# A graph kernel's first gather stage: node features in two strided block loads, edge types as rows that TensorE spreads

## What is computed

```python
# first layer (R=32 types, B=8 basis matrices)
W_rel = einsum('rb,bdf->rdf', w_comp, weight)
agg   = segment_sum(h[src] * norm, etype * n_nodes + dst, 32 * n_nodes)
node  = einsum('rnd,rdf->nf', agg.reshape(32, n_nodes, 128), W_rel) + h_bias + h @ loop_weight
x     = layernorm(x + relu(node))
# second layer: per edge e = (x_dst - x_src) @ theta.T + x_src @ phi.T, batch norm, relu,
# @ fc1.T, batch norm, relu, mean over the edges of a destination, relu(. + x), layernorm
```

## Time and profile before

| | |
|---|---|
| median of 3 runs | 3090.55 us (3073.56 to 3092.17) |
| profiled execution | 3090.62 us |
| its span | 3088.8 us |
| mean granted TensorE clock | 0.712 |
| first gather stage, first gather to last | 11.4 to 1217.3 us |

### The profile page before, as it was taken

How to read it: one execution, slowest core, us unless ns; L and a number is a source line. 1 busy time by engine, 2 the same in 40 slices (tenths; PEclk the granted TensorE clock), 3 DMA queues, 4 the chain that set the end, 5 groups by cost and what they waited for, 6 DMA issues and landing times. The chain is left out here.

```text
span 3088.8 us, 42986 instructions
## 1 busy us (share of the span) xinstructions
PE 1948.1 (63%) x10210; PEld 1494.5 (48%) x10211; DVE 1365.8 (44%) x3584; ACT 614.7 (20%) x1004; POOL 1605.7 (52%) x1759
## 2 busy tenths in 40 slices
PE   2666566656666666635554545445555579999997
PEld 2555465645655556622222222222222234499996
DVE  4333333333433333533333333333333358877776
ACT  2111111111111111411010101010101137534434
POOL 5665665666666664246666666666666620092002
PEclk9778777778778787855555555555555569999999
DMA  3221212121222211223333333333333349534443
GB/s 87 54 55 53 59 51 56 52 60 54 59 59 53 59 54 40 90 86 95 103 99 94 96 95 93 95 108 96 95 94 96 108 178 308 185 121 143 145 149 96
DMA packets 124080, 291.20 MB, mean 94 GB/s; under 512 B 34957, under 2 KB 77506, under 8 KB 106224
## 3 DMA queue, kind: packets, MB, share of 16 engines
q1 hardware_dynamic: 65856, 136.12, 13.5%
q0 software_dynamic: 50048, 102.50, 12.8%
q10 hardware_dynamic: 8112, 51.91, 4.3%
HBM read 227.22 MB, written 63.18 MB: 94 GB/s over the span
## 5 line engine op out<-in xcount | busy, mean ns | idle before, releaser
L697 POOL DMA_INDIRECT G<-btab,srcT x782 | 737.5, 943 | 534.9 <-POOLq L56 278.6
L682 POOL DMA_INDIRECT G<-in_x,srcT x782 | 746.3, 954 | 469.1 <-issue 233.3
L906 PE MATMUL PS<-ident,G 128*128 128x128 f32 x784 | 212.9, 427 | 568.9 <-PEq L56 335.9
L906 PEld LDWEIGHTS PS<-ident,G 128*128 128x128 f32 x784 | 140.1, 217 | 662.5 <-issue 662.5
L791 PE MATMUL PS<-BIG 128*128 128x192 f32 (+1 forms) x1584 | 352.0, 372 | 126.4 <-issue 124.6
L780 PE MATMUL PS<-BIG,G 128*128 128x192 f32 x1564 | 362.9, 393 | 91.2 <-issue 57.6
L791 PEld LDWEIGHTS PS<-BIG 128*128 128x128 f32 x1584 | 312.8, 222 | 152.9 <-issue 152.6
L1477 DVE TENSOR_SCALAR ohT<-PS,node_col 80x512 bf16<-80x512 f32 x196 | 146.2, 746 | 536.6 <-DVEq L56 317.2
L780 PEld LDWEIGHTS PS<-BIG,G 128*128 128x128 f32 x1564 | 328.6, 237 | 105.3 <-issue 104.8
L1046 ACT ACTIVATE BIG<-PS 128x768 f32<-128x768 f32 x196 | 156.3, 809 | 1032.7 <-ACTq L56 887.4
L1313 DVE SCALAR_TENSOR_TENSOR BIG<-PS,dst0T,BIG 128x192 f32<-128x192 f32 x784 | 324.2, 416 | 79.9 <-issue 67.1
(11 more groups left out here) (182 smaller groups left out, 1834.3 us busy)
## 6 DMA issues: line engine op xcount, KB each, us to landing
BIG<-spill SPq DMA_DIRECT2D x90, 1024.0 KB, 4.9
spill<-BIG ACTq DMA_DIRECT2D x49, 1024.0 KB
G<-in_x,srcT POOLq DMA_INDIRECT x782
G<-btab,srcT POOLq DMA_INDIRECT x782
typ_i<-in_edge_type SPq DMA_DIRECT2D x97, 128.0 KB
BIG<-atab SPq DMA_DIRECT2D x196, 60.0 KB
atab<-BIG SPq DMA_DIRECT2D x12, 384.0 KB
xn<-in_x SPq DMA_DIRECT2D x48, 64.0 KB
```

The source lines that it names most:

```text
L682: nc.gpsimd.indirect_dma_start(out=G[0:n, g % 2, t, :], out_offset=None, in_=x, in_offset=bass.IndirectOffsetOnAxis(ap=srcT[0:n, TPG * g + ...
L697: nc.gpsimd.indirect_dma_start(out=G[0:n, g % 2, t, :], out_offset=None, in_=btab[:, :], in_offset=bass.IndirectOffsetOnAxis(ap=srcT[0:n, ...
L906: pe.matmul(PS[:, 2 + k, q * TILE:(q + 1) * TILE], G[:, h, TPC * k + q, :], ident[:, :], start=(q == 0), stop=False, is_transpose=True, sk ...
```

## The change

- **x**: xn is one buffer of 128 nodes. A new tile xh [128, 25, 128] receives x in two loads, blocks 0 to 24 behind the weights' loads in the setup, blocks 25 to 48 when 25 blocks have been used. Partition p holds the nodes 49 p to 49 p + 48, each load takes a contiguous run of each partition's nodes, and block g is therefore the nodes 49 p + g. ScalarE copies block g+1 from xh to xn (`next_x`), behind the copy of the transpose, which moves behind the fourth product's copy. XT and ACC keep their order by node; block g of them is now every 49th column (`every`).
- **edge types**: etype is loaded once as 98 rows beside src, dst and norm, and converted to bf16. TensorE spreads four rows over the 128 partitions by a product with a 0/1 matrix (`spread`, K = 98), 256 columns at a time, two products a group, into bank 7; VectorE makes the one-hots from PSUM, 256 columns at a time, two a group. typ_i and the 97 + 1 broadcast loads are gone.
- **order of TensorE in a group**: scaled sums 0; wait for the second one-hot of the group before (`rel_oh_ready`); [lookup of coefficients, odd groups], basis product 1; wait `loop_done`, first spreading; scaled sums 1; wait for x and for the first one-hot, transpose; basis product 0; loop product; second spreading.
- **order of VectorE**: half 0, first one-hot, half 1, add_loop, second one-hot. The coefficients are scaled in half 0 of the odd group. The lookup uses bank 5 instead of 4.

```diff
@@ SP
-            load_types(0, [ROW] * TPC)
+            def load_x(first, n):
+                for p0, p1 in ((0, EDGEP), (EDGEP, FULLP), (FULLP, P)):
+                    m = min(n, LASTW - first) if p1 == P else n
+                    of = x[p0 * NW + first:p0 * NW + first + m, :].rearrange("(p w) d -> p w d", p=1) if p1 == P else \
+                        x[p0 * NW:p1 * NW, :].rearrange("(p w) d -> p w d", w=NW)[:, first:first + n, :]
+                    sp.dma_start(xh[p0:p1, 0:m, :], of).then_inc(x_in, 16)
...
+            load_x(0, XH)
...
-            with sp.Fori(1, NG // 2 - 1) as i:
-                first_pass(2 * i, 0, i)
-                first_pass(2 * i + 1, 1, i)
...
+            take(sp, xw_free, XH)
+            load_x(XH, NW - XH)
+            sp.wait_ge(x_in, 16 * 6)
+            sp.sem_inc(x_here, NW - XH)
@@ TensorE
+            def spread_types(c, first, bank, at, n):
+                row = spread[:, bass.ds(c * TPC, TPC), :].rearrange("p q r -> p (q r)")
+                return pe.matmul(PS[:, bank, at:at + n], row, types[:, first:first + n], start=True, stop=True, skip_group_check=True)
...
+                    def first_types():
+                        take(pe, loop_done)
+                        spread_types(types_at[0], types_at[1], 7, 2 * P, QUARTER).then_inc(typ_spread, 1)
                     def turn_nodes():
-                        reached(pe, "pe", x_in[h], 16 * (use + 1))
-                        take(pe, loop_done)
-                        pe.transpose(PS[:, 7, 0:P], xn[:, h, 0:D], ident[:, :]).then_inc(xwT_ps, 1)
+                        take(pe, x_ready)
+                        take(pe, loop_done if last(g, NG) else rel_oh_ready)
+                        pe.transpose(PS[:, 7, 0:P], xn[:, :], ident[:, :]).then_inc(xwT_ps, 1)
...
+                    def second_types():
+                        spread_types(types_at[0], types_at[1] + QUARTER, 7, 2 * P, QUARTER).then_inc(loop_ps, 1)
...
                         if not (isinstance(g, int) and g == 0):
-                            basis_product(1, False)
+                            take(pe, rel_oh_ready)
+                            basis_product(1, h == 1)
+                        first_types()
+                        scaled_sums(g, h, use, 1)
                         turn_nodes()
-                        scaled_sums(g, h, use, 1)
-                        basis_product(0, h == 0)
+                        basis_product(0, False)
                         loop_product()
+                        second_types()
@@ ScalarE
-                    if k == (0 if last(g, NG) else 2):
+                    if k == (0 if last(g, NG) else CPG - 1):
                         take(act, xwT_ps)
                         act.sem_inc(xw_free, 1)
-                        act.activation(XT[:, bass.ds(g * TNODES, TNODES)], PS[:, 7, 0:P], ACT.Copy).then_inc(xwT_ready, 1)
+                        act.activation(every(XT, g), PS[:, 7, 0:P], ACT.Copy).then_inc(xwT_ready, 1)
+                        if not last(g, NG):
+                            next_x(g + 1)
@@ VectorE, setup
+            step(dve.tensor_copy(spread[:, :, :], ident[0:NR, 0:(NC + 1) * TPC].rearrange("p (n o) -> p n o", o=1).to_broadcast([NR, (NC + 1) * TPC, R])))
+            dve.wait_ge(wts_in, 16 * 13)
+            step(dve.tensor_scalar(types.rearrange("p (b e) -> p b e", b=TPR), r_typ, 1.0, None, ALU.mult))
@@ VectorE, loop
-            def one_hot_types():
-                take(dve, typ_in, 16 * TPC)
-                step(dve.tensor_scalar(rel_oh, typ_i, rel_col[:, :], None, ALU.is_equal))
+            def one_hot_types(at, of):
+                return dve.tensor_scalar(rel_oh[:, at:at + of.shape[1]], of, rel_col[:, :], None, ALU.is_equal)
...
+                    def types_of(quarter):
+                        if quarter == 0:
+                            take(dve, typ_spread)
+                        one_hot_types((1 - h) * CHUNK + quarter * QUARTER, PS[:, 7, 2 * P:2 * P + QUARTER]).then_inc(rel_oh_ready, 1)
...
+                        types_of(0)
                         half(g, h, use, 1)
                         add_loop()
+                        types_of(1)
```

More of the change, by code:

```diff
@@ L101, in gnn_kernel @@
     TURNS = NG // SLOTS
+    XH = (NW + 1) // 2
+    FULLP = N // NW
+    EDGEP = FULLP // 16 * 16
+    LASTW = N - FULLP * NW
+    assert FULLP == P - 1 and XH <= LASTW < NW and NW == NG
     assert NG % 2 == 1 and NBU % 2 == 1 and NW % 2 == 1
@@ L185, in gnn_kernel @@
         ln_b = sb("ln_b", [P, NWP])
-        xn = sb("xn", [P, 2, WPB * D])
+        xh = sb("xh", [P, XH, D])
+        xn = sb("xn", [P, D])
+        spread = sb("spread", [NR, (NC + 1) * TPC, R], BF16)
         xT = sb("xT", [P, 2, WPB * D])
@@ L219, in gnn_kernel @@
         soh = part(2 * TPP * ZW).rearrange("p (s t k n) -> p s t k n", s=2, t=TPP, k=B)
-        zs = part(2 * TPP * ZW).rearrange("p (s t k n) -> p s t k n", s=2, t=TPP, k=B)
+        zs = part(2 * TPP * ZW)
+        r_typ = zs[0:NR, 0:ROW].bitcast(I32).rearrange("p (b e) -> p b e", b=TPR)
+        zs = zs.rearrange("p (s t k n) -> p s t k n", s=2, t=TPP, k=B)
         sohx = part(ZW).rearrange("p (k n) -> p k n", k=B)
@@ L234, in gnn_kernel @@
         XT = xf
+        types = xT[0:NR, 0, :].bitcast(BF16)
         def rows(of, k, dt=F32):
@@ L522, in further_windows, with every @@
                     body(i)
+        def every(t, g):
+            return t[:, 0:NW * TNODES].rearrange("f (p w) -> f w p", w=NW)[:, bass.ds(g, 1), :].rearrange("f o p -> f (o p)")
         def win(t, w):
@@ L565, in _ @@
             sp.wait_ge(rows_out, 16 * 6)
[L567 to L587 removed]
+            sp.wait_ge(x_in, 16 * 3)
+            sp.sem_inc(x_here, XH)
+            take(sp, xw_free, XH)
+            load_x(XH, NW - XH)
+            sp.wait_ge(x_in, 16 * 6)
+            sp.sem_inc(x_here, NW - XH)
             def store_b(u, s, use):
@@ L812, in one @@
                         tile_windows(pe, g, tile, whole_group)
+                    types_at = (use + 1 + h, (1 - h) * CHUNK)
+                    def first_types():
+                        take(pe, loop_done)
+                        spread_types(types_at[0], types_at[1], 7, 2 * P, QUARTER).then_inc(typ_spread, 1)
                     def turn_nodes():
-                        reached(pe, "pe", x_in[h], 16 * (use + 1))
-                        take(pe, loop_done)
-                        pe.transpose(PS[:, 7, 0:P], xn[:, h, 0:D], ident[:, :]).then_inc(xwT_ps, 1)
+                        take(pe, x_ready)
+                        take(pe, loop_done if last(g, NG) else rel_oh_ready)
+                        pe.transpose(PS[:, 7, 0:P], xn[:, :], ident[:, :]).then_inc(xwT_ps, 1)
                     def loop_product():
                         take(pe, xwT_ready)
-                        pe.matmul(PS[:, 7, P:2 * P], loop_s[:, :], XT[:, bass.ds(g * TNODES, TNODES)], start=True, stop=True).then_inc(loop_ps, 1)
+                        return pe.matmul(PS[:, 7, P:2 * P], loop_s[:, :], every(XT, g), start=True, stop=True)
+                    def second_types():
+                        spread_types(types_at[0], types_at[1] + QUARTER, 7, 2 * P, QUARTER).then_inc(loop_ps, 1)
                     if last(g, NG):
+                        take(pe, rel_oh_ready)
                         scaled_sums(g, h, use, 0, (0,))
@@ L1197, in step @@
                 take(dve, dve_self)
-            for r, fill in ((r_src, 0), (r_dst, -1), (r_nrm, 0.0)):
+            for r, fill in ((r_src, 0), (r_dst, -1), (r_nrm, 0.0), (r_typ, 0)):
                 dve.memset(r.rearrange("p b e -> p (b e)")[WHOLE:NR, LEDGE:ROW], fill).then_inc(pads_set, 1)
@@ L1349, in half @@
                     more = not last(g, NG)
-                    if more and h == 0 and p == 0:
-                        one_hot_types()
                     if not first:
@@ L1354, in half @@
                         take(dve, seg_ready)
-                        if more and h == 0 and p == 1:
+                        if more and h == 1 and p == 0:
                             scale_coef(use + 1)
@@ L1372, in add_loop @@
                     def add_loop():
-                        acc = ACC[:, bass.ds(g * TNODES, TNODES)]
+                        acc = every(accf, g)
                         take(dve, loop_ps)
```

69 lines of the change are left out of this document (26 added, 43 removed).

## The result

The change makes the kernel slower by 0.8%: 3108.72 us in the median of 14 runs (3098.56 to 3114.24), against 3083.28 us for the kernel before in 14 runs beside it (3073.56 to 3097.35); ratio 1.0079, 95% interval 1.0061 to 1.0096. The profiled execution took 3105.04 us with a span of 3103.0, which is 14.4 us more than the profiled one of before (span 14.2 us more).

What follows compares the result with a forecast made beforehand. No engine is full; GpSimd's 782 gathers (974 us) plus pauses for chunks handed back late (211 us) set the first stage. Gathers -7, pauses +14, start +2, tail +8 give +17 on 3090.6: 3108 us, range 3062 to 3155.

Steps and rivals of the forecast that it cites:

- the circle: New waits make TensorE and VectorE wait for each other in turn: 16.6 us a group at full clock, against 10.7.
- Small loads: Removing 97 type broadcasts and 49 x loads from SP's queue in the gather stage: 0 us, range 0 to -20.
- rival B: Removed DMAs and SP instructions free the instruction budget, so GpSimd pauses less: 59 pauses, -31 us, total 3063 us; chance 0.18.
- Gathers no longer lengthened: First stage: GpSimd's gathers no longer slowed by VectorE's one-hots from SBUF, 24 pairs x 0.28 us: -7 us.
- Strided accesses: XT and ACC accessed at every 49th element: at most +0.3 us on each of three operations a group.
- The 7 us that lead to 3115: By the skill's rule on 16-byte lines alone, strided accesses would add rival A's +7 us to the forecast.
- Pauses: GpSimd's waits in the first stage for a chunk handed back: +14 us, 0 to +44, from +7 instructions and +7 crawl.
- one budget of instructions a run: Engines' slow issue beside gathers begins after a number of instructions; 6.5 more a group, +3.3%, give +7 us of pauses.
- one of time with +44 us: Slow issue begins after some 12.2 us of fast work a run; a slower group then means pauses x 1.21, +44 us.
- rival A: The circle sets the pace: +44 us for pauses, +7 for strided operations, +54 in all, 3145 us; chance 0.28.
- Start: Before the first chunk is handed back at 68 us: one-hots from PSUM cost more, +2 us (0 to +4).
- Tail: Behind the last gather, groups 47 and 48, nothing hides the circle's waits: +8 us (+4 to +13).

Runs made afterwards that it cites:

- no type loads: Kernel before without the loop's small type loads, every pair looked up from the first pair's types: 3079.73 us, ratio 0.9992.
- x alone: Kernel before with only the change's x half (xh, two big loads, every 49th column), types and order as before: 3093.58 us, ratio 1.0032.
- no circle: Changed kernel with second x load one group earlier, spreading and one-hots moved so one of four waits a pair is left: 3080.51 us, ratio 1.0011 to before.
- long ScalarE: Kernel before with four long ScalarE operations, 3.2 us of work, added behind each group's last copy: 3082.73 us, ratio 1.0016.
- SP's instructions: Kernel before with 32 more semaphore instructions a group on SP, which nobody waits for: 3078.52 us, ratio 1.0018.
- plain x: The no circle kernel with x loaded as before, by small contiguous loads of 128 nodes a group: 3105.45 us, ratio 1.0026 to the kernel before.
- strided: Kernel before, x loaded as it is, but XT written and read and ACC added at every 49th column: 3097.02 us, ratio 1.0003.
- types alone: Changed kernel with x by 49 small loads as before, so only types spread by TensorE, new order and waits: 3107.14 us, ratio 1.0088 to before.
- waits alone: Kernel before with only the changed order and two waits (before basis product 1 and the transpose), no other computation: 3119.11 us, ratio 1.0124.
- early x: Changed kernel with the second load of x issued one group earlier: 3113.91 us, ratio 1.0135 to the kernel before.

## Why the prediction was right, and where not

The sign was right and the time hit to a microsecond, but that much agreement is luck. The forecast was +17 us on a base of 3090.6, a ratio of 1.0055; measured are +25.4 us on 3083.28, and 1.0055 lies below the interval (1.0061 to 1.0096). The base was 7 us too high and the difference 8 us too small. Beside its single profile, all kernels of the study now give each term a sample: eight without the circle or with one wait of it (before, no type loads, x alone, no circle, long ScalarE, SP's instructions, plain x, strided) and four with all of it (the change, types alone, waits alone, early x).

- **Small loads, 0.** Right: 0.9992 without the types' loads, and rival B fell with it: those 97 loads gone, 71 pauses. With x's 49 loads gone instead the pauses were 64 but longer, 219 us.
- **Gathers no longer lengthened, -7.** Right in kind, 4.8 us measured: GpSimd's busy time went from 713.78 to 709.08 for the same 750 gathers, and the longest gather of the stage from 1.47 to 0.96 us. The price was read from one gather, and 0.28 for 0.75 us is no partial lock-out: that gather started 0.35 us into the one-hot. In the stage before, 20 gathers started under a one-hot of types, and 19 of them took longer by what was left of it less 0.12 to 0.13 us (one was not lengthened). Early in the stage, for instance, 0.58 us were left and the gather took 0.45 more:

```profile
70.98 0.75 DVE L1287 TENSOR_SCALAR BIG<-typ_i,rel_col 128x1024 bf16<-128x1024 int32 x1 [4.64 <-issue]
...
71.16 1.39 POOL L682 DMA_INDIRECT G<-in_x,srcT  x1 [0.30 <-issue]
```

  Over all one-hots of the stage that makes 6.5 us.
- **Strided accesses, 0 to +0.3 each.** +0.09 for the addition, +0.13 for the copy of the transpose, +0.06 for a record of the loop product, and nothing in the kernel's time. The Trainium skill, SBUF — State Buffer, § Door 1: The DMA port swizzle, has the sign of these. The 7 us that lead to 3115 are not borne out: they would be a ratio of 1.0023, and the accesses alone give 1.0003 (0.9989 to 1.0017).
- **Pauses, +14.** The size was about right: 223 us in pauses in the mean of the four kernels with the circle, 207 in that of the eight without, +16; +19 in the change itself. The failed step is how it comes about. The prediction had pauses of one length and asked for their number, "the pauses follow the instructions", +3.3% in number. They went from 71 to 90 in those means, +27%, and became shorter (2.35 us for 2.90 in the change). The text had two readings, one budget of instructions a run, and one of time with +44 us. Both took the crawl as what ends each run, and neither saw that with the change the crawl would end few of them: crawls fell from 348 to 122 us of the stage, and only 13 of 92 pauses have one ahead of them. The timeline shows the circle ending one run; that it ends most of the others is argued. That would be rival A's mechanism at less than half of its price (16 to 19 us of pauses, not 44). Why it stayed cheap is open. That the displaced crawl had cost nearly as much is one reading, but the kernel without the circle lost 100 us of crawl and no pause time; no run takes the crawl away by itself.
- **Instructions as a budget.** Not borne out for SP's 32 a group; ScalarE's 131 us of added busy time do nothing either. What starts a crawl is open. Short instructions added to ScalarE, which would test a budget of the three engines alone, were not tried.
- **Start, +2.** Wrong in sign: -10.0, and the prediction had named 5 us here as a sign of being wrong. All five kernels that spread the types resume at 58.7 to 60.1 us, the nine with typ_i at 66.2 to 69.0. Timeline of the kernel after, where the earlier trace rows had the wait of 12.40:

```profile
39.87 0.80 PE L769 MATMUL PS<-BIG 128*128 128x32 bf16 x24 [3.27 <-PEq L56]
...
43.85 0.75 DVE L1317 TENSOR_SCALAR BIG<-PS,rel_col 128x512 bf16<-128x512 f32 x1 [4.13 <-DVEq L56]
44.52 0.42 DVE L1322 TENSOR_TENSOR BIG<-PS,normT 128x256 f32<-128x256 f32 x1
...
46.91 2.69 DVE L1344 SCALAR_TENSOR_TENSOR BIG<-PS,dst0T,BIG 128x192 f32<-128x192 f32 x8 [0.26 <-issue]
```

  The crawl that made L1294 wait from 44.93 to 57.33 does not occur there; the first scaled hots start at 46.91, not 59.72. The prediction said "thaw decides" and took the crawl of this one place as given, although part of the work ahead of it was to change. The loads of x are not what keeps it away: types alone loads x as before and resumes at 58.8 us, x alone has the two large loads and resumes at 68.0. Which part of the types' half does it (no load of typ_i at the start, the one-hots in two operations from PSUM, the lookup's earlier place) was not tried.
- **Tail, +8.** This term was too small by half: +12.8 in the change, +14 between the two means (41.5 and 27.7), and the lower of these still has two kernels with one wait in it (33.5 and 33.7). The waits were well put; what was missed is that with them TensorE no longer runs at full clock:

```profile
1229.41 0.77 PE L769 MATMUL PS<-BIG 128*128 128x32 bf16 x24 [2.87 <-PEq L56]
1230.03 4.48 PE L800 MATMUL PS<-BIG 128*128 128x192 f32 x16
...
1240.35 0.45 PE L831 MATMUL PS<-ident,xn 128*128 128x128 f32 x1 [3.13 <-PEq L56]
1240.59 4.27 PE L800 MATMUL PS<-BIG 128*128 128x192 f32 x16
...
1251.21 2.90 PE L789 MATMUL PS<-BIG,G 128*128 128x192 f32 x8 [5.79 <-PEq L56]
1253.90 4.41 PE L800 MATMUL PS<-BIG 128*128 128x192 f32 x16
```

  Waits of 2.87, 3.13 and 5.79 us make 11.8, though not all of that is on top of before; and three basis products take 4.3 to 4.5 us, against 2.76 in the earlier trace rows at the same place: 4.9 more.

Summed by these means, the circle costs 16 + 14 = 30 us, the start gives back 10 and the gathers 5: +15. The means mix in the two kernels with one wait left. A cleaner comparison is that of the three kernels that spread the types and have all waits (the change, types alone, early x) with the six that have neither (before, no type loads, x alone, long ScalarE, SP's instructions, strided): start -8.8, stage +14.0 (pauses +14.3, gathers -5.3, other idle time for the rest), tail +16.2, all behind the second stage +1.6. That is +23.0, of the medians' +25.4. Against it the sum was off by -11 at the start, +7 in the stage, whose terms came to +7, and +8 in the tail. These misses partly cancel; what they leave, 6 us here and 8 by the medians, the base made up for, which was 7 us too high.

The kernel without the circle and its pair with plain x fit in: they start the stage 8.3 us earlier than the six and end it with a tail 7.8 us longer.

No version of the study beats the kernel before. The best that has all of the change's operations, the one with a single wait left, is level with it. A kernel with no wait of this kind at all was not made.

## What to carry to other kernels

When a change shares one small buffer (here bank 7) between two engines and so makes each wait for the other's last piece of work, price the waits, not only the operations: here order and waits alone cost 1.2%, and the kernel with all of the change's operations and one wait of four cost nothing measurable. Look at each wait's place, since its length says little: 257 us of waits cost 1.23% in one kernel, 326 us 0.11% in another. And look at the end of the stage, where no other limit hides a wait: of 30 us lost in stage and tail together, 16 were in the tail. When the present limit is a stall that has its own rhythm, a second limit does not simply add to it or hide beneath it: the pauses became 27% more and shorter, and their sum grew by 14 to 19 us where the two simple readings had 7 and 44.

## What the runs showed of the hardware that was not expected

While gathers run, the other engines at times issue each instruction only after 0.4 to 1.8 us of idle time. This is not tied to SP's instructions (32 more a group: 71 pauses, 201 us) nor to ScalarE's busy time (131 us more: 71 pauses, 202 us). By the count above it took 348 us of the stage before, 246 to 286 with new waits alone or with spread types and one wait, and 122 to 134 with the types spread and all the waits. What starts it is open.

A gather that GpSimd starts under VectorE's one-hot of 128x1024 from SBUF is longer by what is left of the one-hot less 0.12 to 0.13 us (19 of 20 in the stage before, up to 1.47 us for 0.94); beside the one-hots of 128x256 from PSUM no gather took over 0.96 us.

And two kernels whose TensorE waits equally long (260 and 257 us on L56) cost 0.45% and 1.23%, by where the wait stands.
